# Two banks for the attended rows, another slot table, and the last batch finished in two halves of tiles

## The reference

```
mod = silu(c) @ wmod                     # sa, ca, ga, sb, cb, gb for each batch
h = layernorm(x) * (1 + ca) + sa
q, k, v = split(h @ w_qkv + b_qkv)
x = x + ga * (softmax(q k^T * scale + band mask) v @ w_out + b_out)
h = layernorm(x) * (1 + cb) + sb
scores = sigmoid(h @ gate_w.T)           # 4 of 8 groups by the sum of their best 2, then the best 8 of 64
w = 2.5 * picked scores / their sum
pos = running count of each expert's tokens, kept while pos < 256
y = (silu(buf @ w_gate) * (buf @ w_up)) @ w_down        # buf: the rows of each expert
out = x + gb * sum over a token's experts of w * y
```

## Time and profile before

| | us |
|---|---|
| median of 3 runs (984.01 to 989.56) | 989.44 |
| the profiled execution | 989.2 |
| its span, first to last instruction | 987.5 |
| PE, DVE, POOL, ACT busy | 719.3, 544.6, 643.2, 373.7 |

### The profile page before, as it was taken

The page is one execution under the profiler, slowest core; times in us unless marked ns, Lnnn a source line. Parts: engine busy times, 40 slices in busy tenths (PEclk is TensorE's granted clock), DMA queues, the critical chain, the costliest instruction groups (busy, mean ns, idle before and its releaser), DMA issues.

```text
span 987.5 us, 15482 instructions
## 1 busy us (share of the span) xinstructions
PE 719.3 (73%) x4732; PEld 470.7 (48%) x4732; DVE 544.6 (55%) x1974; ACT 373.7 (38%) x827; POOL 643.2 (65%) x592
## 2 busy tenths in 40 slices
PE   4579998997997897989988861200899998888200
PEld 3235555554554564554455530200788777666100
DVE  3566569779869878778678772600222222222038
ACT  2135654544444455445444530000344333333100
POOL 5206332687786886886885656776388888887630
PEclk9879998998987998898898976555899999999755
DMA  8695996275466446534526379100999999898878
GB/s 306 162 341 159 333 336 189 82 251 180 172 202 227 151 157 212 181 101 162 172 97 201 115 227 282 37 5 4 247 277 276 263 231 159 162 161 182 216 211 332
DMA packets 165134, 191.60 MB, mean 194 GB/s; under 512 B 21497, under 2 KB 146581, under 8 KB 165052
## 3 DMA queue, kind: packets, MB, share of 16 engines
q1 hardware_dynamic: 128636, 134.27, 42.7%
q0 software_dynamic: 30720, 38.03, 18.8%
q10 hardware_dynamic: 5696, 18.30, 5.2%
HBM read 100.77 MB, written 110.67 MB: 214 GB/s over the span
## 4 chain that ended last, share of the span: by engine, by line
PE 36%; DVE 20%; POOL 15%; DMA 12%; issue 11%; SPq 3%; ACT 2%; POOLq 0%; DVEq 0%; ACTq 0%
POOL acc_d L725 8%; DMA acc_d<-ys,xg 7%; PE stageA L952 6%; POOL slots_d L642 5%; PE outT L1022 4%; PE scores L980 4%; PE scoresT L1181 4%; DVE junk L1249 4%; PE scoresT L1002 4%; PE scoresT L1006 3%; PE stageA L962 2%; DVE pairs L1313 2%; PE stageC L1077 2%; DVE sc L1313 1%; PE stageC L1059 1%
## 5 line engine op out<-in xcount | busy, mean ns | idle before, releaser
L642 POOL DMA_INDIRECT slots_d<-H,dest x256 | 259.1, 1012 | 95.0 <-issue 57.4
L725 POOL DMA_INDIRECT acc_d<-ys,xg x128 | 198.4, 1550 | 60.3 <-issue 29.8
L1249 DVE CUSTOM_DVE_ANT_0 junk<-scores,mask 128x256 bf16<-128x256 f32 x512 | 187.6, 419 | 76.1 <-PE scores L980 75.8
L779 ACT ACTIVATE PT<-scoresT 128x512 f32<-128x512 f32 (+1 forms) x320 | 152.8, 508 | 140.7 <-PE scoresT L1006 137.1
L1181 PE MATMUL scoresT<-xgT,wgu 128*128 128x256 f32 x512 | 127.6, 393 | 23.0 <-ACT xgT L873 22.8
L1002 PE MATMUL scoresT<-mask,identb 128*128 128x512 bf16 (+1 forms) x320 | 116.5, 364 | 19.8 <-DMA Qs<-MT 14.3
L980 PE MATMUL scores<-Ks,Qs 96*128 96x256 bf16 x512 | 108.5, 298 | 30.4 <-DVE mrowmax L1249 26.6
L1181 PEld LDWEIGHTS scoresT<-xgT,wgu 128*128 128x128 f32 x512 | 96.1, 194 | 48.3 <-ACT xgT L873 35.3
L1006 PE MATMUL scoresT<-Qs,Ks 98*128 98x256 bf16 (+1 forms) x640 | 117.1, 267 | 0.0
L1022 PE MATMUL outT<-PT,Va 128*32 128x256 f32 (+1 forms) x1280 | 94.9, 370 | 0.0
L596 POOL TENSOR_TENSOR r<-p,parts 128x512 f32<-128x512 f32 x32 | 39.3, 1227 | 78.7 <-ACT parts L771 77.2
(11 more groups left out here) (195 smaller groups left out, 1179.5 us busy)
## 6 DMA issues: line engine op xcount, KB each, us to landing
xg<-slots_d SPq DMA_DIRECT2D x64, 324.0 KB, 4.4
slots_d<-blank ACTq DMA_DIRECT2D x26, 648.0 KB, 5.1
parts_d<-parts SPq DMA_DIRECT2D x32, 384.0 KB, 2.7
Qs<-parts_d SPq DMA_DIRECT2D x96, 128.0 KB
Ks<-parts_d SPq DMA_DIRECT2D x90, 128.0 KB
acc_d<-zero SPq DMA_DIRECT2D x32, 272.0 KB
wgu<-L_ffn_w_gate_dram SPq DMA_DIRECT2D x64, 128.0 KB, 3.2
wgu<-L_ffn_w_up_dram SPq DMA_DIRECT2D x64, 128.0 KB, 3.3
```

The lines of the kernel that those rows point to most:

```text
L642: pool.indirect_dma_start(out=slots_d[:, :], in_=H2[bt.par][:, t, :], in_offset=None, out_offset=bass.IndirectOffsetOnAxis(ap=dest[bt.par] ...
L725: pool.indirect_dma_start(out=acc_d[ACC[e]][:, :], in_=ys[e % NY][:, h, :], in_offset=None, out_offset=bass.IndirectOffsetOnAxis(ap=xg[e % ...
L779: sc_.activation(PT[m % NPT][:, :, 0:w], src, ACT.Exp).then_inc(sems["exp"], 1)
L1249: ins = v.tensor_tensor_reduce(out=junk[:, i, :], in0=bS[n % 2][:, i * 2 * P:(i + 1) * 2 * P], in1=mask[:, edge, :], scale=1.0, scalar=TAK ...
```

## The change

1. **The slot table.** `stats` of batch b + 2 moves from slots 9 and 10 to slots 8 and 10. `onT` goes from slots 2 and 3 to 2 and 2, `op` from 4 and 5 to 3 and 3, `x1` from 4 and 5 to 3 and 4, `stats2` from 5 and 5 to 4 and 5, and `norm2` from 7 and 7 to 7 and 8. These hold for bodies 1 to 6 (`stats` for 0 to 5).
2. **Two banks.** `PAIR = (bC, bA)`: the two parts of `onT` and of `op` use stageC and stageA in turn, so that the second part doesn't wait for the first to be taken out. The projection that comes to stageA next waits for `t1` instead.
3. **Body 7 has a table of its own**, `LAST`, with all stages of batch 6 some slots earlier (its key in slot 15 and not 19). `SEND_LAST` sends batch 5's rows at two per slot in slots 0 to 15, `SEND_SELF` the first 8 of batch 6 in slots 16 to 19. Batch 7's `load_c` moves from behind body 7 to slot 10 and its `c_xb` to slot 13.
4. **The last batch in halves.** After body 7, `c_rstd`, `c_xhat`, `c_norm`, the turn, the logits, routing, count and key are done for tiles 0 and 1, then for tiles 2 and 3. The 16 sends of a half wait only for that half. `c_xs` of this batch is done by DVE, into `xc`, and stored from there.

```diff
-    load_x=(-14,), stats=(-11, -10), a_rstd=(-9,), a_norm=(-6,), a_mod=(-9,), hT=(-4, -3), proj=(-2, -1, 7, 8),
+    load_x=(-14,), stats=(-12, -10), a_rstd=(-9,), a_norm=(-6,), a_mod=(-9,), hT=(-4, -3), proj=(-2, -1, 7, 8),
     split=(-1, 0, 0, 1, 1, 2, 8, 8, 9, 9, 10, 10), store=(1, 3, 10, 11), stack=(4, 12), v=(9, 11, 12),
-    xb=(2,), onT=(2, 3), op=(4, 5), x1=(4, 5), x1_store=(10,), xs=(11,), stats2=(5, 5), c_rstd=(5,), xhat=(6,), norm2=(7, 7),
+    xb=(2,), onT=(2, 2), op=(3, 3), x1=(3, 4), x1_store=(10,), xs=(11,), stats2=(4, 5), c_rstd=(5,), xhat=(6,), norm2=(7, 8),
     h2T=(8, 9), lg=(10,), route=(11, 12, 12, 13, 13, 14, 15, 15, 16, 17, 18, 18), cnt=(18,), key=(19,), zero=(3,),
...
+LAST = dict(
+    xb=(1,), onT=(2, 2), op=(3, 3), x1=(3, 4), x1_store=(9,), xs=(8,), stats2=(4, 4), c_rstd=(4,), xhat=(5,), norm2=(6, 6),
+    h2T=(7, 7), lg=(8,), route=(8, 9, 9, 10, 10, 11, 11, 12, 13, 13, 14, 14), cnt=(14,), key=(15,), zero=(3,),
+    load_c=(10,), xb_self=(13,),
+)
+def at(name, slot, now=None):
+    return [k for k, s in enumerate((LAST if now and now.b == B - 1 else AT)[name]) if s == slot]
...
+SEND_LAST = {SLOTS + slot: 2 for slot in range(16)}
+SEND_SELF = {slot: 2 for slot in range(16, 20)}
+def sends(now, slot):
+    table = SEND if now.b < B - 1 else SEND_LAST
+    return sum(n for s, n in table.items() if s < SLOTS + slot), table.get(SLOTS + slot, 0)
...
 ROUTE_PARTS = [0, 3, 7, 11, 14, 17, 20, 23, 27, 31, 32, 36, 38]
+HALVES = (slice(0, T // 2), slice(T // 2, T))
+HALF_PARTS = [0, 3, 7, 11, 14, 17, 20, 23, 27, 27, 28, 32, 34]
...
+        PAIR = (bC, bA)
+        LATE = dict(onT=(bA, bST[0]), op=(bST[1], bO), h2T=(bA, bST[0]), lg=(bC, bST[1]), cnt=(bT, bO))
...
                         store_x1(prev)
                     if not nxt and slot >= 1:
                         early_w(now, slot)
+                    for _ in at("load_c", slot, now) if not nxt else []:
+                        load_c(now)
...
             load_stack(first, 1)
             batches(body)
             last = batch(B - 1)
-            load_c(last)
             rows = slots_d.rearrange("(h p e) c -> p h e c", h=2, p=P)
...
-            store_x1(last)
+            store_x1(last, xc)
...
-            def c_rstd(bt):
-                after(pool, "aggr2", bt, T)
+            def c_rstd(bt, ts=slice(0, T), done=0):
+                after(pool, "aggr2", bt, ts.stop)
...
             def send(bt, i):
-                if i == 0:
+                if bt.b == B - 1 and i % (T * K // 2) == 0:
+                    half = i // (T * K // 2)
+                    after(pool, "key", bt, 2 * half + 2)
+                    after(pool, "idc", bt, half + 1)
+                    after(pool, "route", bt, HALF_PARTS[-1] * (half + 1))
+                    after(pool, "h2", bt, 2 * half + 2)
...
             def send_some(bt, now, slot, part):
-                n = SEND.get(SLOTS + slot, 0)
+                first, n = sends(now, slot)
                 mine = range(0, n, 2) if part == 0 else range(1, n, 2)
                 if mine:
-                    after(pool, "exp", now, 2 * slot + part)
+                    after(pool, "exp", now, 2 * slot + part - (2 if now.b == B - 1 else 0))
                 for i in mine:
-                    send(bt, SENT_BEFORE[SLOTS + slot] + (i // 2 if part == 0 else (n + 1) // 2 + i // 2))
+                    send(bt, first + (i // 2 if part == 0 else (n + 1) // 2 + i // 2))
...
+                    if not nxt:
+                        for _ in at("xb_self", slot, now):
+                            c_xb(now)
+                        for i in range(SEND_SELF.get(slot, 0)):
+                            send(prev, sum(n for s, n in SEND_SELF.items() if s < slot) + i)
...
             batches(body)
             last = batch(B - 1)
             pre = batch(B - 2)
-            c_xb(last)
-            for i in range(10):
+            ready = sum(SEND_SELF.values())
+            for i in range(ready, ready + 6):
                 send(pre, i)
-            c_rstd(last)
-            c_xs(last)
-            for i in range(10, T * K):
+            c_rstd(last, HALVES[0])
+            send(pre, ready + 6)
+            c_rstd(last, HALVES[1], 4)
+            for i in range(ready + 7, T * K):
                 send(pre, i)
             for i in range(T * K):
                 send(last, i)
...
                     for bt, j in steps("proj", now, slot):
                         a_p32(bt, j)
-                    for k in at("onT", slot) if prev else []:
-                        c_onT(prev, k)
-                    for _ in at("xhat", slot) if prev else []:
+                    for k in at("onT", slot, now) if prev else []:
+                        c_onT(prev, k, PAIR[k])
+                    for _ in at("xhat", slot, now) if prev else []:
                         c_xhat(prev)
-                    for k in at("h2T", slot) if prev else []:
-                        c_h2T(prev, k)
...
+                    for k in at("h2T", slot, now) if prev else []:
+                        c_h2T(prev, k, bC if nxt else PAIR[k])
...
+            def half_xhat(half):
+                after(act, "h2Tp", last, 0)
+                after(act, "rstd2", last, 4 * half + 4)
+                for t in range(T)[HALVES[half]]:
+                    sc_.activation(H2[last.par][:, t, 0:D], x1[:, t, :], ACT.Identity, scale=rs2[:, t:t + 1],
+                                   bias=nmean2[:, t:t + 1]).then_inc(sems["xn2"], 1)
...
+            def half_ex(half):
+                after(act, "lg", last, half + 1)
+                after(act, "route", last, 0)
+                w = T * E // 2
+                sc_.activation(ex[:, half * w:(half + 1) * w], LATE["lg"][half][:, 0:w], ACT.Exp, scale=-1.0
+                               ).then_inc(sems["ex"], 1)
+            need(act, sent[last.par], 16 * T * K * (last.b // 2))
+            half_xhat(0)
+            half_xhat(1)
+            half_h2T(0)
+            half_ex(0)
+            half_h2T(1)
+            half_ex(1)
...
+                if j == 2 and bt.b >= 2:
+                    after(pe, "t1", batch(bt.b - 2), 2)
                 f = TURN[j]
...
             def c_onT(bt, k, bank=bC):
                 after(pe, "on", bt, QUADS)
-                if bank is bC and k == 0:
+                if bt.b < B - 1 and bank is bC:
                     after(pe, "key", bt, -1)
-                elif bank is bC:
-                    after(pe, "onT", bt, k)
+                elif bt.b < B - 2:
+                    after(pe, "p32", batch(bt.b + 2), 2)
+                elif bt.b == B - 2:
+                    after(pe, "v", batch(B), 0)
...
                 after(pe, "onT", bt, C)
-                if bank is bC:
-                    after(pe, "t1", bt, n)
...
             def c_h2T(bt, k, bank=bC):
                 after(pe, "h2", bt, 2)
-                if bank is bC and k == 0:
+                if k == 0 or bank is bA:
                     after(pe, "t1", bt, 2)
                 elif bank is bC:
                     after(pe, "h2T", bt, k)
...
-            for k in range(C):
-                c_h2T(last, k, LATE["h2T"][k])
+            def half_h2T(half):
+                after(pe, "h2", last, 2 * half + 2)
+                for k in range(C):
+                    for i, t in enumerate(range(T)[HALVES[half]]):
+                        at = (2 * k + i) * P
+                        turned = nc.tensor.transpose(LATE["h2T"][half][:, at:at + P],
+                                                     H2[last.par][:, t, k * P:(k + 1) * P], ident[:])
+                turned.then_inc(sems["h2Tp"], 1)
...
+            def half_cnt(half):
+                after(pe, "pre", last, (4, T + 2)[half] - 1)
+                bank, w = LATE["cnt"][half], T * E // 2
+                mm(bank[:, 0:w], before[:], selb[:, half * w:(half + 1) * w], start=True, stop=False)
+                mm(bank[:, 0:w], onesb[0:1, :], enum[:, 0:w], start=False, stop=False)
+                mm(bank[:, 0:w], ones64[:], Spre[:, HALVES[half], :].rearrange("p t e -> p (t e)"), start=False, stop=True
+                   ).then_inc(sems["cntp"], 1)
+            half_h2T(0)
             after(pe, "key", last, -1)
-            c_lg(last)
-            e_cnt(last, LATE["cnt"])
+            half_lg(0)
+            half_h2T(1)
+            half_lg(1)
+            half_cnt(0)
+            half_cnt(1)
...
+                    after(pe, "key", batch(B - 1), 4)
...
                 c_x1(last, n, LATE["op"][n])
                 c_stats(last, n)
-            c_norm(last, 0)
-            c_norm(last, 1)
-            for k in range(12):
-                c_route(last, k)
-            e_key(last, LATE["cnt"])
+            for half, ts in enumerate(HALVES):
+                c_norm(last, 0, ts, 2 * half)
+                c_norm(last, 1, ts, 2 * half)
+            v.tensor_tensor(xc[:], x1[:], mr[:, 3, :].unsqueeze(1).to_broadcast([P, T, D]), ALU.mult
+                            ).then_inc(sems["xs"], 1)
```

(27 more changed lines are left out.)

168 lines of the change are left out of this document (89 added, 79 removed).

## The result

The changed kernel takes 1009.08 us (median of four runs, 1005.29 to 1011.57), the kernel before 986.73 us (four runs): a ratio of 1.0225, 95% interval 1.0171 to 1.0279. The forecast was 1008, worked out from a kernel before of 989.4 us; against the 986.73 us here the loss is 22.4 us where 19 were forecast. The profiled execution's span is 1007.3 us where it was 987.5, so 19.8 us are to be found in the traces.

What follows compares the result with a forecast made beforehand. POOL's send queue was taken to bound the stretch behind the attention, where no engine leads throughout. 987.5 - 16.9 + 28.6 + 7.5 + 0 = 1006.7, plus 1.7 outside the span, called 1008 us; 8-in-10 range 974 to 1018.

Steps and rivals of the forecast that it cites:

- The wait for x: Slot 8, bodies 1 to 5: statistics wait for x before the second norm product, delaying PE's c_h2T(0); +28.6 us.
- The clock: PE after the new stalls in bodies 1 to 5: half speed at first, 1.5 us per body, +7.5 us.
- The closer stages: Two banks and earlier onT, op, x1: 0 us, bounds -1.5 and +1.5 for body 6.
- I take nothing off: Bodies 1 to 5: PE's delay reaches DVE whole, so none of the 28.6 us is taken back.
- rival 2: Bodies 1 to 5: 2 to 4 of each 5.7 us stall come back, total 982 to 997 us; chance 0.20.
- The queue: POOL's 96 sends of batches 5 to 7 behind the attention: 139.3 us from 156.2, -16.9 us.
- no wait for `mr`: POOL's queue: mr is loaded ten slots earlier, so its 6.58 us of idle time goes.
- no wait for batch 7's key: Tail: first half's key at 623 to 628, before POOL reaches batch 7's first send at 631.2.
- The idle time left: POOL's queue after the change: 1.3 us, left for a shorter wait for mv.
- It is POOL and not the attention that sets this stretch: Body 7: POOL's 62 us of sends and larger steps exceed the 55 us to the attention's end.
- The key chain: Batch 7's norm to key: taking c_xs from POOL also gives it about 2 us.
- the wait of `x1` for `xc`: Body 6, slot 3: first x1 waits for xc before slot 4's maxima; H's chain can't begin before 475.6.

Runs made afterwards that it cites:

- Run 2: Changed kernel with both norm products in slot 7 again and the statistics left in slot 8: 986.08 us, ratio 1.0001 to the kernel before.
- run 9: The plain changed kernel measured again on chip C: 1008.75 us, ratio 1.0236 to the kernel before.
- Run 10: Changed kernel with ten unread matmuls on PE before c_h2T(0)'s wait for H in bodies 1 to 5, on chip C: 1005.62 us, ratio 1.0188.
- run 6: Changed kernel without its closer onT, op and x1, on chip B: 1034.28 us, ratio 1.0263 to the kernel before.
- run 7: Changed kernel with ten unread matmuls on PE before c_h2T(0)'s wait for H in bodies 1 to 5, on chip B: 1037.19 us, ratio 1.0264.
- run 1: Changed kernel with the statistics of xt put back in slots 9 and 10: 987.07 us, ratio 0.9998 to the kernel before.
- run 4: Changed kernel with the earlier slot table for bodies 1 to 6, keeping the two banks, body 7's table and the halves: 974.97 us, ratio 0.9884.

## Why the prediction was right

**The wait for x, +28.6 forecast, 29.7 measured** as the delay of PE's turn over five bodies. The mechanism is as argued: the landing is fixed by SP's queue (26.9 to 33.0 us from the start of a body wherever DVE is seen waiting for it, over all traces), the second product stands behind it, PE behind that. That SP's queue sets the landing is read from the order of its loads; no run moved the load. Run 2 shows that it goes through `H`: with the product in front of the block the loss of 22 us is gone. Undoing the step gives back 22 us and not these 29.7, with the clock on top, because the cost of the closer stages then appears.

**The clock, +7.5 forecast; 8.1 measured on the spot** (1.5 to 1.7 us in each body from the first to the second part of the turn), but given back. This is where a step failed, "I take nothing off": bodies 1 to 5 are longer by 32.1 us and not by 29.7 + 8.1 = 37.8, so 5.7 us come back in slots 10 to 19 (run 9's trace of the same kernel has 26.9 us of delays and bodies 1 to 5 longer by 28.4, so both numbers are good to some 4 us). That is rival 2 at a small size. Run 10 points the same way in sum, but its time leaves it undecided, so that DVE, the later one there, takes up what the clock cost is argued and not shown. The rule of the Trainium skill (TensorE: Matmul & The Clock Gate, HAM oscillation — how this bites in real kernels) that a burst of matmuls behind a long wait starts throttled agrees with the row of 1.12 us at 378.02, where the granted clock is 0.50. Not every wait did it: behind 1.49 us in body 1 of run 9 the turn took 0.66 us and the second part came 3.88 us later. The rule foretells the slow stretch, not whether the slow stretch ends last.

**The queue, -16.9 forecast, -12.9 measured** over the 96 sends. The steps in it were right: no wait for `mr`, none for `H`, no wait for batch 7's key. The idle time left was mis-sized, 1.3 us against 1.97 + 3.00. The 3.00 us is a wait that I had not priced: body 7 is 64.1 us long and not 55, so batch 6's own key is late for the sends behind it. Of the 9.1 us, 6.8 lie in the second quad (23.8 against 17.0), where batch 6's routing now begins: DVE's first routing step waits 4.69 us for ACT's `ex` at 593.94, and behind it PE waits 4.41 us for the maxima at 599.68. That the earlier routing is the whole cause was not tried. "It is POOL and not the attention that sets this stretch" was true for all but those 3 us. The key chain gained as expected from `c_xs` leaving POOL: the norm products, 4.50 us in sum beside it, take 2 x 1.42 = 2.84 us at 642.32 and 646.15.

**The closer stages, 0 forecast.** In the changed kernel that holds: body 6, which has no x to wait for, is 0.6 us longer, and run 6 against run 7 shows 2.0 us over bodies 1 to 6. But the reason was only half given. I named the wait of `x1` for `xc` in front of slot 4's maxima and set it against a gain between the halves. There was no gain to see in the first quad: it is 3.8 us longer. Over bodies 1 to 6 half of that comes back later in the body, 9.4 us stay in the traces of runs 1 and 4 and 12 us in their times, and in the changed kernel the wait for x hid it. Undoing the visible stall, as in run 1, brings it out. Body 6 is no proof that the stages are free: its first quad is 4.3 us longer (15.9 against 11.7) and its second 4.2 us shorter.

So the two errors that count, 4 us too much gained by the queue and 4 us too much lost by the stalls, cancel. That the sum came out closer than its terms is luck.

## What to carry to other kernels

Before moving a step into another's place in an in-order queue, ask for each engine what stands behind it: the statistics themselves take 1 us, and the product that came to stand behind their wait cost 22 over five bodies. Price each part alone as well as in the whole, since a stall that sets the end hides the cost of everything in front of it: here the closer stages cost 2 us or less while the stall was there and 12 us once it was gone. Where one engine's queue sets the end, count its instructions and take out waits and steps; that part of the change gives 1.2 to 1.4% alone on two chips of three.
